# Perceiver block, first two stages: the first pair's folds issued ahead of the turned tokens, the norm in two halves, and a store wait moved by four tiles

## The reference

```python
def cross(hidden_q, kv_c, Wq, w_kc_q, w_kc_kv, W_qr, W_kr, Wo):
    q_hk = (hidden_q @ Wq.T).reshape(b, s, H, K)             # H=16, K=128
    q_big = einsum('bshk,hkq->bshq', q_hk, w_kc_q)           # 384 wide
    kv_rope = kv_c * cos + rotate_half(kv_c) * sin
    q_r = einsum('bshq,hqr->bhsr', q_big, W_qr)              # R=64
    k_r = einsum('bld,hdr->bhlr', kv_rope, W_kr)
    attn = softmax(einsum('bhsr,bhlr->bhsl', q_r, k_r))
    ctx_c = einsum('bhsl,bld->bhsd', attn, kv_rope)
    return (einsum('bhsd,hkd->bshk', ctx_c, w_kc_kv)).reshape(b, s, H * K) @ Wo.T

x = x + cross(layernorm(x), ctx_512, ...)
x = x + self_attention(layernorm(x), ...)
x = x + mixture_of_experts(layernorm(x), ...)
```

## Time and profile before

| what | value |
|---|---|
| median of 3 runs | 1462.76 us (1459.79 to 1463.19) |
| profiled execution, its own time | 1460.57 us |
| its span, first to last instruction | 1458.7 us |
| PE busy share of the span | 92% |
| mean granted clock of PE | 0.969 of full |

### The profile page before, as it was taken

The page is one execution under the profiler, slowest core; times in us unless marked ns, Lnnn a source line. Parts: engine busy times, 40 slices in busy tenths (PEclk is TensorE's granted clock), DMA queues, the critical chain, the costliest instruction groups (busy, mean ns, idle before and its releaser), DMA issues. The chain is left out here.

```text
span 1458.7 us, 22813 instructions
## 1 busy us (share of the span) xinstructions
PE 1348.2 (92%) x7136; PEld 1107.0 (76%) x7136; DVE 792.5 (54%) x1387; ACT 729.3 (50%) x1736; POOL 549.7 (38%) x336
## 2 busy tenths in 40 slices
PE   5999799999999999999997999998899989999991
PEld 4777577878787878787875888887678768787781
DVE  4444466666666666656664444445388833432245
ACT  2444466565656555655554777777222223333330
POOL 2430233233231415151113333334034396228975
PEclk9999899999999999999998999999899999999996
DMA  5786422141415151513041333532643266546767
GB/s 197 257 271 207 166 102 102 62 170 50 180 43 187 43 187 43 187 43 115 1 173 63 106 109 109 165 115 95 233 153 121 80 223 202 177 129 215 249 193 223
DMA packets 78984, 209.66 MB, mean 144 GB/s; under 512 B 5888, under 2 KB 39168, under 8 KB 72960
## 3 DMA queue, kind: packets, MB, share of 16 engines
q1 hardware_dynamic: 69472, 163.65, 32.2%
q0 software_dynamic: 7136, 38.80, 7.9%
q10 hardware_dynamic: 2304, 6.29, 1.1%
HBM read 154.46 MB, written 92.01 MB: 169 GB/s over the span
## 5 line engine op out<-in xcount | busy, mean ns | idle before, releaser
L787 DVE TENSOR_TENSOR probsT_lo<-psTr,probsT_hi 128x512 fp32r<-128x512 f32 x256 | 176.6, 690 | 166.1 <-ACT probsT_hi L740 165.8
L740 ACT CAST probsT_hi<-psTr 128x512 fp32r<-128x512 f32 x256 | 150.2, 587 | 197.6 <-PE psTr L874 193.9
L874 PE MATMUL psTr<-ident,probs 128*128 128x128 f32 x1024 | 153.7, 274 | 12.0 <-DVE probsT_lo L787 5.9
L874 PEld LDWEIGHTS psTr<-ident,probs 128*128 128x128 f32 x1024 | 124.4, 141 | 51.6 <-DVE probsT_lo L787 14.6
L782 DVE TENSOR_REDUCE nmax<-psS 128x1 f32<-128x1024 f32 x128 | 155.3, 1214 | 14.0 <-DMA qe<-stage 7.3
L696 ACT ACTIVATE probs<-psS,nmax 128x1024 f32<-128x1024 f32 x128 | 143.8, 1123 | 14.9 <-DVE nmax L782 14.9
L652 POOL TENSOR_TENSOR w_slots<-ctx_f,w_slots 128x512 fp32r<-128x512 f32 x32 | 41.4, 1294 | 279.4 <-ACT w_slots L703 279.4
L79 PE MATMUL psS<-w_slots 128*128 128x512 f32 x256 | 113.5, 443 | 6.6 <-ACT probs L696 4.7
L79 PE MATMUL psV<-probsT_hi,w_slots 128*128 128x512 f32 x256 | 114.8, 448 | 0.7
L79 PE MATMUL bank<-w_slots,ao_first_hi 128*128 (+1 forms) x244 | 104.3, 427 | 5.8 <-POOL w_slots L1618 3.0
L81 PE MATMUL psS<-w_slots 128*128 128x512 f32 x256 | 103.0, 402 | 0.0
(11 more groups left out here) (300 smaller groups left out, 3275.1 us busy)
## 6 DMA issues: line engine op xcount, KB each, us to landing
w_ahead<-w_exp POOLq DMA_DIRECT2D x14, 1536.0 KB, 7.4
qe<-stage SPq DMA_DIRECT2D x16, 1024.0 KB, 6.8
w_slots<-qe SPq DMA_DIRECT2D x15, 1024.0 KB, 4.9
wraw<-w_pairs SPq DMA_DIRECT2D x8, 1792.0 KB, 11.3
early<-xs SPq DMA_DIRECT2D x47, 256.0 KB, 2.8
xs<-h_rows SPq DMA_DIRECT2D x47, 256.0 KB, 2.1
early<-ctx SPq DMA_DIRECT2D x16, 512.0 KB, 9.7
ao<-attn_out SPq DMA_DIRECT2D x32, 256.0 KB, 2.9
```

The lines of the kernel that those rows point to most:

```text
L740: act.copy(PT[k % PTN].hi[:], psT[slot][:]).then_inc(turned_hi, 1)
L787: dve.tensor_tensor(out, psT[slot][:], f32(hi), ALU.subtract).then_inc(turned_free, 1)
L874: last = pe.transpose(psT[slot][:, q * P:(q + 1) * P], src(q), ident[:])
```

## The change

1. Loads: `x` tiles 0 to 3, then the W_A part of pair 0's weights alone (1088 KB, its own semaphore `wA_in`), then `x` tiles 4 to 7, then the W_B part, then pair 1. One transfer more than before, on the same queue.
2. PE: `fold_t` of pair 0 stands ahead of token tile 0, `fold_c` after tile 1 (`C_AT` = 1). ACT's copies of both follow the same order.
3. Norm: the statistics of tiles 0 to 3, their `var` and `rstd`, and their four normalised tiles come first; those of tiles 4 to 7 after it. POOL computes two powers of four values instead of one of eight.
4. Four row buffers `h`, and four banks for the turned tiles (`psE` and `psF`, two each) in place of `psQ` and `psE`: tile tt now waits for tile tt - 4.
5. Cross stage: the wait for the stores moves on DVE from ahead of the first four `maxes` to behind them, and ACT gets the same wait behind the first four `exps`. The write of `probs` and `nmax` no longer waits for the stores, the write of the turned probabilities does.

The diff, cut to its core:

```diff
-    T_AT, C_AT = 4, 6
+    TH, C_AT = 4, 1
...
-    h = [sb(f"h1_{j}", [P, D]) for j in range(2)]
+    h = [sb(f"h1_{j}", [P, D]) for j in range(TH)]
...
+    psH = [psE[:, 0], psE[:, 1], psF[:, 0], psF[:, 1]]
...
     @block.sync
...
-        for j in range(2):
-            sp.dma_start(raw[j][:], w_pairs[j]).then_inc(w_in[j], 16)
+        load_x(0)
+        load_x(1)
+        sp.dma_start(raw[0][:, 0:W_A], w_pairs[0, :, 0:W_A]).then_inc(wA_in, 16)
+        load_x(2)
+        load_x(3)
+        sp.dma_start(raw[0][:, W_A:], w_pairs[0, :, W_A:]).then_inc(w_in[0], 16)
+        sp.dma_start(raw[1][:], w_pairs[1]).then_inc(w_in[1], 16)
...
     @block.gpsimd
-        pool.wait_ge(ln1, NT + NT + 1)
-        pool.tensor_tensor(rstd[:], var[:], eps_pow[:, 0:1].to_broadcast([P, NT]),
-                           ALU.pow).then_inc(rstd1, 1)
+        for a in range(2):
+            part = slice(a * TH, (a + 1) * TH)
+            pool.wait_ge(ln1, (2 * TH + 1) * (a + 1))
+            pool.tensor_tensor(rstd[:, part], var[:, part], eps_pow[:, 0:1].to_broadcast([P, TH]),
+                               ALU.pow).then_inc(rstd1, 1)
...
     @block.vector
-        dve.wait_ge(rstd1, 1)
-        for tt in range(2):
-            norm(tt)
-        for tt in range(NT):
...
-            if tt + 2 < NT:
-                norm(tt + 2)
-            if tt == C_AT:
+        stats(0)
+        dve.wait_ge(rstd1, 1)
+        for tt in range(TH):
+            norm(tt)
+        stats(1)
+        turned_low(0)
+        turned_low(1)
+        dve.wait_ge(rstd1, 2)
+        for tt in range(TH, NT):
+            norm(tt)
+            if tt == TH + 1:
                 fold_c(0)
+            if tt % 2:
+                turned_low(tt - 3)
+                turned_low(tt - 2)
+        turned_low(NT - 2)
+        turned_low(NT - 1)
...
     @block.tensor
+        pe.wait_ge(wA_in, 16)
+        fold_t(0)
         for tt in range(NT):
             pe.wait_ge(h1_made, tt + 1)
-            if tt >= 2:
-                pe.wait_ge(h1_lo, tt - 1)
+            if tt >= TH:
+                pe.wait_ge(h1_lo, tt - TH + 1)
...
             last.then_inc(h1_turned, 1)
-            if tt == T_AT:
-                fold_t(0, 1)
             if tt == C_AT:
                 fold_c(0, 0)
...
 build_cross, ACT:
         for rt in range(RT):
             exps(0, 0, rt)
+        act.wait_ge(stage_out, 32 * (NP + 1))
...
 build_cross, DVE:
-        dve.wait_ge(stage_out, 32 * (NP + 1))
         for rt in range(RT):
             maxes(0, 0, rt)
+        dve.wait_ge(stage_out, 32 * (NP + 1))
```

More of the change, by code:

```diff
@@ L177, in build_queries @@
     x_in = [sem(f"x_in{a}") for a in range(XP)]
-    w_in = [sem(f"w_in{j}") for j in range(2)]
+    w_in, wA_in = [sem(f"w_in{j}") for j in range(2)], sem("wA_in")
     const_set, ln1, rstd1, h1_made = sem("const_set"), sem("ln1"), sem("rstd1"), sem("h1_made")
@@ L207, in _, with load_x @@
     def _(sp):
-        for a in range(XP):
+        def load_x(a):
             part = slice(a * NT // XP, (a + 1) * NT // XP)
             sp.dma_start(x_all[:, part, :], x_d[part].rearrange("t p c -> p t c")).then_inc(x_in[a], 16)
-        for j in range(2):
-            sp.dma_start(raw[j][:], w_pairs[j]).then_inc(w_in[j], 16)
+        load_x(0)
[5 more added lines that the diff above has]
+        sp.dma_start(raw[1][:], w_pairs[1]).then_inc(w_in[1], 16)
         sp.dma_start(keep["rope_tab"], t["rope_x"]).then_inc(keep["tab_in"], 16)
@@ L286, in _ @@
             act.copy(h1T.hi[:, :, tt * P:(tt + 1) * P],
-                     (psE if tt % 2 else psQ)[:, 0, :].rearrange("p (k t) -> p k t", k=KC)).then_inc(h1_hi, 1)
-            if tt == T_AT:
-                fold_t(0)
+                     psH[tt % TH].rearrange("p (k t) -> p k t", k=KC)).then_inc(h1_hi, 1)
             if tt == C_AT:
@@ L333, in _, with stats @@
         dve.sem_inc(f_free, 2)
-        for tt in range(NT):
[L335 to L340, removed]
+        def stats(a):
+            part = slice(a * TH, (a + 1) * TH)
+            for tt in range(a * TH, (a + 1) * TH):
+                dve.wait_ge(x_in[tt * XP // NT], 16)
+                dve.bn_stats(st[:, tt, :], x_all[:, tt, :]).then_inc(ln1, 1)
+                dve.wait_ge(ln1, 2 * tt + 1 + a)
+                dve.bn_aggr(mv[:, tt, :], st[:, tt, :]).then_inc(ln1, 1)
+            dve.wait_ge(ln1, 2 * TH * (a + 1) + a)
+            dve.tensor_scalar(var[:, part], mv[:, part, 1], EPS, None, ALU.add).then_inc(ln1, 1)
         def norm(tt):
-            if tt >= 2:
-                dve.wait_ge(h1_turned, tt - 1)
-            dve.tensor_scalar(h[tt % 2][:], x_all[:, tt, :], mv[:, tt, 0:1], rstd[:, tt:tt + 1],
+            if tt >= TH:
+                dve.wait_ge(h1_turned, tt - TH + 1)
+            dve.tensor_scalar(h[tt % TH][:], x_all[:, tt, :], mv[:, tt, 0:1], rstd[:, tt:tt + 1],
                               ALU.subtract, ALU.mult).then_inc(h1_made, 1)
@@ L351, in fold_c, with turned_low @@
                               f32(C.hi[:].rearrange("p k m -> p (k m)")), ALU.subtract).then_inc(c_ready, 1)
-        dve.wait_ge(rstd1, 1)
-        for tt in range(2):
-            norm(tt)
-        for tt in range(NT):
+        def turned_low(tt):
             dve.wait_ge(h1_hi, tt + 1)
             dst = slice(tt * P, (tt + 1) * P)
-            dve.tensor_tensor(h1T.lo[:, :, dst], (psE if tt % 2 else psQ)[:, 0, :].rearrange("p (k t) -> p k t", k=KC),
+            dve.tensor_tensor(h1T.lo[:, :, dst], psH[tt % TH].rearrange("p (k t) -> p k t", k=KC),
                               f32(h1T.hi[:, :, dst]), ALU.subtract).then_inc(h1_lo, 1)
-            if tt + 2 < NT:
-                norm(tt + 2)
-            if tt == C_AT:
-                fold_c(0)
+        stats(0)
[9 more added lines that the diff above has]
+            if tt == TH + 1:
+                fold_c(0)
+            if tt % 2:
[3 more added lines that the diff above has]
+        turned_low(NT - 1)
         def key_low(q):
@@ L406, in _, with fold_t @@
         pe.wait_ge(const_set, 3)
-        def fold_t(j, n):
-            pe.wait_ge(w_in[j], 16 * n)
+        def fold_t(j):
             for jj in range(2):
@@ L422, in fold_c @@
             last.then_inc(c_mm, 1)
+        pe.wait_ge(wA_in, 16)
+        fold_t(0)
         for tt in range(NT):
             pe.wait_ge(h1_made, tt + 1)
-            if tt >= 2:
-                pe.wait_ge(h1_lo, tt - 1)
+            if tt >= TH:
+                pe.wait_ge(h1_lo, tt - TH + 1)
             for k in range(KC):
-                last = pe.transpose((psE if tt % 2 else psQ)[:, 0, k * P:(k + 1) * P],
-                                    h[tt % 2][:, k * P:(k + 1) * P], ident[:])
+                last = pe.transpose(psH[tt % TH][:, k * P:(k + 1) * P],
+                                    h[tt % TH][:, k * P:(k + 1) * P], ident[:])
             last.then_inc(h1_turned, 1)
-            if tt == T_AT:
-                fold_t(0, 1)
             if tt == C_AT:
@@ L453, in step @@
             if ahead:
-                fold_t(1 - j, n)
+                pe.wait_ge(w_in[1 - j], 16 * n)
+                fold_t(1 - j)
             else:
```

## The result

Measured: median 1443.66 us (1441.12 to 1446.65, 4 runs) against 1461.4 us of the kernel before (4 runs); ratio 0.9876, 95% interval 0.9847 to 0.9905. Between the medians that is 17.7 us less where I had forecast 12.6. A later comparison of the same two kernels with more runs gave 0.9896 (0.9879 to 0.9912), which is 15.2 us less than 1459.74, with 12.9 to 17.7 as its bounds.

The account below looks back on a forecast made before the run. PE was taken to wait in the opening and to bound the pairs loop, with a stand at the cross stage. Opening 7.1 plus seam 5.5 made 12.6 us less, forecast 1449.5 us, range 1446 to 1455.

Parts of the forecast that it names:

- The opening: Stretch before the pairs loop: the loop's first matmul would come at 23.5 instead of 30.57 us, 7.1 us earlier.
- the power of four: POOL's power of four values in the opening's norm: taken as 1.1 us, where the power of eight takes 1.69.
- Four buffers and banks cost nothing: Opening's row buffers and tile banks: no added time, as no tile waits for a bank.
- the price of all the opening's PE work at the lower clock: Opening: all PE matmuls priced at the earlier rows' lower level, 1.2 GHz, twice their later time.
- The seam: Cross stage's start, first score matmul to first turn: 5.5 us saved by moving the store wait.
- the upper of my two cases: Cross stage's start with PE's clock at full rate: first turn at 160.7 instead of 166.49, 5.8 us earlier.
- The new wait on ACT: Cross stage, behind the four exponentials at 160.5, long after the stores landed at 156.07: costs nothing.
- the load of the queries: Cross stage: next quarter's queries land at 161.0, just before their scores at 161.1, capping any further gain.
- from the sum to the time: Whole kernel: 12.6 us off the profiled 1460.57 gives 1448.0, or 1450.2 by the median 1462.76; forecast stated as 1449.5.
- The rival of a clock that rises within the opening: Opening: the second fold, tiles behind it and first eight loop matmuls at full rate, 3 us more, 1446.5; chance 0.04.
- The 8.5 us without a gap before did not do it: Opening: argument against the rising clock, from PE working nearly without a gap from 20.45 to 28.98 at the lower level.
- The other rivals: W_A late 1453.5, 0.08; one part not paying about 1456, 0.06; no change 1461, 0.04; slow clock into loop 1467, 0.03.

Follow-up runs that it names:

- the first piece alone: Changed kernel with W_A loaded in two transfers, the first fold's 1152 columns ahead of the second's 1024: 1446.71 us, ratio 0.9906 to the kernel before.
- the opening alone: Changed kernel with DVE's store wait put back ahead of the first four maxima, keeping the opening's changes: 1450.15 us, ratio 0.9933 to the kernel before.
- changed_d: Fourth profile of the changed kernel, no edit: loop's first matmul at 21.94 us, span 1443.2 us.
- the run with one norm: Changed kernel with one norm over all eight tiles instead of halves, early folds and four buffers kept: loop at 27.98 us, span 1451.8 us.

## Why the prediction was right or wrong

**The opening** was right in its steps and its size: 7.1 us forecast, 7.05 between the means of the profiles (7.65 in the first pair). Landing of W_A, both folds, the power of four and the last tiles came within 0.6 us of the working, and the experiments showed PE's list from the landing on as what carries it (loads in the old order: loop 2.9 us later for a first fold 2.7 us later; the first piece alone: 1.0 earlier for 1.2). "Four buffers and banks cost nothing" was right; I did not say that they are needed, which they are, for 1.0 to 2.1 us of the opening. One term was mis-sized, though little: the price of all the opening's PE work at the lower clock, as said below.

**The seam** was right in mechanism and slightly small: 5.5 forecast, 5.8 measured, the upper of my two cases, in which the clock is at its higher level from score tile 2 on, as it was in the changed profiles (0.39 us for a 128x512 matmul behind that tile's first). The new wait on ACT cost nothing, and the load of the queries is what is late next.

**The pairs loop** kept its length (118.4 and 118.5 on average), so nothing was taken back. W_B and its first splits stayed covered: PE goes from pair 1's first fold to `psE` in 1.37 us before and after.

**The step that failed is the one from the sum to the time: "Against the profiled execution's own 1460.57: 1448.0. The median of the runs is 1462.76, 2.2 above it, so 1450.2 by that. I say 1449.5".** I took one execution, and a median of three, as the fixed time of the kernel before. 1449.5 and a gain of 12.6 put that time at 1462.1; sixteen runs gave 1459.74. That is 2.4 of the 5.8 us between forecast and result. With the same gain off 1459.74 the forecast is 1447.1, and the same range begins at 1443.6, where the result lies at its very edge. That median was not the only thing that moved. In profiles of the same kernel the self stage spread by 2.6 us, the pairs loop by 3.7 and the last stage by 2.9, and the profile that I read had the longest last stage and the longest span of its kernel's three. The prediction itself says that a median of three moves by some 0.2%, which is 2.9 us, and used it for the chances only: the range held the unknown prices of the change and left this out.

**The size.** The other 3.5 us are the gain: 16.1 between the medians of the later runs, 15.2 by their ratio, where my sum had 12.6. The timed gain of 15.2 (12.9 to 17.7) holds the 13.6 between the spans' means and the 12.9 of the two parts; my 12.6 lies just outside. Part of the remaining 2 us may be real: the opening alone gave 9.8 in its timed runs and 6.8 in its profile. No stage behind the opening was shorter in all the profiles that share it, so where those 2 us would lie is open.

**The rival of a clock that rises within the opening** took place in part. "The 8.5 us without a gap before did not do it" rested on one profile: the clock rose within the second fold in both further profiles of the kernel before. In the changed kernel it rose ahead of the last two tiles in all four profiles (in `changed_d` within the second fold, in the others during tiles 4 and 5), and in two of them the loop's first matmuls ran at the higher level too. What the two together are worth is read from PE's first row of pair 1's first fold, which stands behind the loop's first 24 matmuls: in the kernel before, in the first changed profile and in the second.

```profile
37.71 1.45 PE L411 MATMUL psT<-wraw 128*128 128x64 f32 x12
29.97 1.45 PE L431 MATMUL psT<-wraw 128*128 128x64 f32 x12
28.77 1.45 PE L431 MATMUL psT<-wraw 128*128 128x64 f32 x12
```

The means of the two kernels there are 36.96 and 29.08, 7.9 us apart where the loop's start is 7.05 apart. That 0.8 us is what I had given the rival 3 us for; later in the loop it is lost again in the scatter.

**The other rivals** did not take place: W_A landed in turn (8.5 to 8.8 in the four changed profiles, forecast 8.65), neither part was taken back, both gains arrived, and the slow start of the loop did not get longer (7.1 us for its first 24 matmuls before, 5.6 to 7.05 after).

## What to carry to other kernels

Where a matrix engine waits for a norm over the first tiles, give it the work that needs only weights, load just the columns of that work next, and split the norm so that the other engines' waits for the delayed inputs fall into work of their own: by the rows here the order of loads pays only together with the halves. A wait that protects memory belongs in front of the first instruction that writes that memory, not at the top of the stage. And before a range is made from one profile, the time of the kernel before and the stages that the change does not touch need a spread of their own: here that of a single stage was as large as a quarter of the gain.

## What the hardware showed that I had not expected

PE's clock rose at different places of the opening from execution to execution, with the same instructions: in one profile of the kernel before not until the loop, in the two others within the second fold. The timeline of PE in the third profile of the kernel before, whose second fold takes 2.34 us where the earlier trace rows has 3.51:

```profile
24.65 2.34 PE L420 MATMUL psC<-tw,wraw 128*128 128x64 f32 x16
26.82 0.61 PE L429 MATMUL psE<-ident,h 128*128 128x128 f32 x4
29.17 0.79 PE L79 MATMUL psQ<-w_slots,cfold_hi 128*128 128x512 f32 x1 [1.74 <-DVE w_slots L359]
```

The tile behind it takes 0.61 instead of 1.06, and after a stand of 1.74 us the loop's matmuls are slow again. In the run with one norm the rise came in the midst of transposes, where the loop then started at full rate. PE's timeline there:

```profile
21.04 1.91 PE L446 MATMUL psF<-ident,h 128*128 128x128 f32 x8
22.75 1.91 PE L446 MATMUL psE<-ident,h 128*128 128x128 f32 x8
24.81 1.42 PE L446 MATMUL psF<-ident,h 128*128 128x128 f32 x8
...
27.98 0.49 PE L79 MATMUL psQ<-w_slots,cfold_hi 128*128 128x512 f32 x1 [1.74 <-DVE w_slots L363]
```

Here too PE stands 1.74 us ahead of the loop, and the loop's first matmul takes 0.49 us instead of 0.79. So the length of the stand alone does not decide the level behind it; the changed kernel stood 1.92 us in all four profiles, and its loop began slow in two and fast in two.

The prediction cited a rule by which nothing would rise in this opening. The Trainium skill, TensorE: Matmul & The Clock Gate, Part 4: PE-mode transpose, says that the full clock does not engage for transposes, since they don't count as busy in the same way. The first half does not hold for the 128x128 transposes of f32 here. PE's rows in `changed_d`, eight of them at each level:

```profile
11.17 1.91 PE L451 MATMUL psE<-ident,h 128*128 128x128 f32 x8
...
16.35 1.04 PE L451 MATMUL psE<-ident,h 128*128 128x128 f32 x8
```

Whether transposes help to raise the clock is suggested but not shown: in the run with one norm it rose among them, with nothing else on PE since 21.04, but the second fold had ended only there.

The granted clock of a row is to be read with care ahead of its first change. The earlier trace rows gives 1.00 for the opening, and the same view gives 1.00 for 30.57 to 33.70 of the kernel before, whose 128x512 matmuls take 0.63 us; in the first changed profile it gives 0.50 for 22.80 to 26.10, where they take 0.63 too. So "its mean clock is 0.96" counts the loop's slow start as full.

Between profiles of one kernel all this shifts the start of the loop by 1.3 to 1.4 us (29.17 to 30.57 before, 21.94 to 23.20 after, of which 0.3 is W_A's landing).
